# An own instruction order for the last of 32 periods in a windowed-attention block (one core, Trainium2)

## The reference, cut to what matters

```python
x = x + attention(_gn(x), ...)            # _gn: group norm, 32 groups, no affine part
# inside attention, 12 heads of 64:
qkv = x @ qkv_w.T + qkv_b                 # plus low-rank terms on q and v
attn = einsum('bqd,bkd->bqk', q * scale, k) + rel_h + rel_w     # 196 x 196 for each head
out = softmax(attn) @ v
return out @ proj_w.T + proj_b            # 768 -> 768, the output projection
```

## Time and profile before

| | |
|---|---|
| time, median of 3 runs | 3322.74 us (3322.59 to 3323.21) |
| the profiled execution | 3322.35 us |
| its span in the trace | 3320.5 us |
| PE busy | 3203.9 us, 96% of the span |
| DVE busy | 2750.2 us, 83% |
| ACT busy | 2124.7 us, 64% |
| mean granted TensorE clock | 0.981 |

### The profile page before, as it was taken

One profiled execution on the slowest core, in us unless ns is written; L12 is line 12 of the kernel. 1 busy time (PEld: TensorE's weight loads), 2 busy tenths in 40 slices (PEclk: granted clock), 3 DMA queues, 4 the chain that ended last, 5 costly groups with the idle time before them and its releaser, 6 DMA issues.

```text
span 3320.5 us, 78578 instructions
## 1 busy us (share of the span) xinstructions
PE 3203.9 (96%) x31280; PEld 1999.0 (60%) x31280; DVE 2750.2 (83%) x5490; ACT 2124.7 (64%) x5491; POOL 35.2 (1%) x65
## 2 busy tenths in 40 slices
PE   7489999999999999999999999999999999999997
PEld 4255666666666666666666666666666666666664
DVE  7688888888888888888888888888888888888874
ACT  3366666666666666666666666666666666666663
POOL 0100000000000000000000000000000000000000
PEclk6799999999999999999999999999999999999999
DMA  3157766567766666776666777666677666677654
GB/s 130 39 107 136 140 126 120 124 132 137 143 139 118 121 124 128 149 140 123 120 127 130 139 143 134 120 120 128 128 148 140 123 117 127 130 141 143 124 103 101
DMA packets 1267533, 420.09 MB, mean 127 GB/s; under 512 B 1092824, under 2 KB 1247448, under 8 KB 1267168
## 3 DMA queue, kind: packets, MB, share of 16 engines
q1 hardware_dynamic: 1251334, 377.69, 59.3%
q10 hardware_dynamic: 15834, 37.37, 3.8%
HBM read 86.60 MB, written 38.54 MB: 38 GB/s over the span
## 4 chain that ended last, share of the span: by engine, by line
PE 64%; DVE 22%; ACT 7%; issue 3%; DMA 1%; SPq 0%; POOL 0%; DVEq 0%; ACTq 0%; POOLq 0%
PE ring L554 34%; PE ring L621 14%; PE score L597 6%; DVE split L801 5%; ACT prob L686 5%; PE o_ps L611 5%; DVE sums L821 3%; DVE row_max L779 3%; PE ring L576 3%; PE ring L627 2%; DVE split L793 1%; DVE x_sb L845 1%; DVE k_lo L746 1%; DVE rel_sb L772 1%; DVE v_split L754 1%
## 5 line engine op out<-in xcount | busy, mean ns | idle before, releaser
L554 PE MATMUL ring<-xn,w_hi 128*128 128x392 f16 x6912 | 1713.0, 329 | 12.9 <-DMA xn<-xs 12.5
L554 PE MATMUL ring<-xn,w_lo 128*128 128x392 f16 x3456 | 1133.6, 328 | 0.0
L686 ACT ACTIVATE prob<-score,neg_max,exp_scale 98x196 f32<-98x196 f32 x1536 | 769.9, 510 | 306.4 <-DVE neg_max L783 303.2
L554 PEld LDWEIGHTS ring<-xn,w_hi 128*128 128x128 f16 x6912 | 643.1, 96 | 482.6 <-DMA xn<-xs 11.9
L801 DVE SCALAR_TENSOR_TENSOR split<-prob,row_inv,split 98x196 f16<-98x196 f32 x1536 | 545.6, 418 | 8.9
L779 DVE TENSOR_REDUCE row_max<-score 98x4 f32<-98x784 f32 x384 | 372.2, 969 | 165.4 <-PE score L597 165.3
L554 PEld LDWEIGHTS ring<-xn,w_lo 128*128 128x128 f16 x3456 | 331.8, 96 | 244.2 <-issue 2.9
L621 PE MATMUL ring<-o_hi,w_hi 128*128 128x392 f16 x1152 | 380.6, 330 | 1.4 <-DVE o_lo L810 1.4
L621 PE MATMUL ring<-o_hi,w_lo 128*128 128x392 f16 x1152 | 379.7, 330 | 0.0
L621 PE MATMUL ring<-o_lo,w_hi 128*128 128x392 f16 x1152 | 379.7, 330 | 0.0
L696 ACT ACTIVATE split<-prob,row_inv 98x196 f16<-98x196 f32 x768 | 310.2, 454 | 72.3 <-DVE row_inv L787 71.5
(11 more groups left out here) (114 smaller groups left out, 4494.8 us busy)
## 6 DMA issues: line engine op xcount, KB each, us to landing
y_sb<-in_x SPq DMA_DIRECT2D x192, 196.0 KB
out<-y_sb SPq DMA_DIRECT2D x192, 196.0 KB
x_sb<-in_x ACTq DMA_DIRECT2D x31, 1176.0 KB
rel_q<-rel_sb SPq DMA_DIRECT2D x128, 122.5 KB, 2.3
stage<-in_L_conv_qkv_w SPq DMA_DIRECT2D x3, 2304.0 KB, 15.0
turned<-split SPq DMA_TRANSPOSE x384, 4.2
rel_q<-rel_sb SPq DMA_DIRECT2D x128, 24.5 KB, 2.1
v_tok<-v_split SPq DMA_TRANSPOSE x192, 3.7
```

The lines of the kernel that those rows point to most:

```text
L554: last = T.matmul(ring[:, bank, 0:NT], w[:, c, 128 * j:128 * j + 128], xn[:, par, xx, :, c, 0:HALF], start=(c == 0 and part == 0), stop=(c ...
L686: last = A.activation(prob[:, head, half, :], score[0:HALF, head, TOK * half:TOK * half + TOK], ACT.Exp, bias=neg_max[:, k % 2, i:i + 1], ...
```

## The change

The last period with scores gets its own four tables (`PE_LAST`, `ACT_LAST`, `DVE_LAST`, `SP_LAST`), and periods 32 and 33 are gone.

1. `Y 3`, `Y 4`, `Y 5` of pair 30 move from slots 9, 10 and 11 to slots 4, 5 and 6, and `Z 3`, `Z 4`, `Z 5` to slots 5, 6 and 7. `V 5` moves from slot 10 and `K 5` from slot 9 to slot 8.
2. `Y` of pair 31 is cut in 36 pieces of three matmuls, `YC` with index 6 c + k: c is the head pair (the block that is summed over), k the output block. A piece waits for `o_lo` of its own head pair alone. Pieces of c = 0 to 4 and k = 0 to 4 (25 of them) stand in slots 9 to 11 and after `P 10`. Those of k = 5 follow, and those of c = 5 after `P 11`, with the transposes `Z` between them.
3. Blocks 0 to 4 use the five ring banks, block 5 and the first `Z` the two banks of `score`, the other `Z` the bank of the block before.
4. There are two buffers for the transposes' input: `yT`, and a part of `xs`, which is idle then.
5. For pair 31, x is loaded once as a whole to `x_sb` (step `LL`, 1176 KB, issued by ACT in slot 4); `Z` adds into it and the stores go out from there. Its six `LY` are gone.

```diff
+def chunks(c):
+    return [("YC", 0, 6 * c + k) for k in range(5)]
+PE_LAST = (
...
+    + each("S", 0, 4) + each("P", 0, 2) + each("Z", 1, 2) + each("K", 0, 3) + each("Y", 1, 3)
+    + each("S", 0, 5) + each("P", 0, 3) + each("V", 0, 3) + each("Y", 1, 4) + each("Z", 1, 3)
...
+    + each("S", 0, 11) + each("P", 0, 9) + chunks(3) + each("P", 0, 10) + chunks(4)
+    + each("YC", 0, 5, 11, 17, 23, 29)
+    + each("P", 0, 11) + each("YC", 0, 30, 31) + each("Z", 0, 0) + each("YC", 0, 32) + each("Z", 0, 1)
...
-    return [(kind, q - old, k) for q in range(-2, pairs + 2) for kind, old, k in order if 0 <= q - old < pairs]
+    return [(kind, q - old, k) for q in range(-2, pairs) for kind, old, k in (order if q < pairs - 1 else last)
+            if 0 <= q - old < pairs]
...
+    end = pairs - 1
+    bank["Y", end, CT - 1] = BANKS
+    bank["Z", end, 0] = BANKS + 1
+    for k in range(1, CT):
+        bank["Z", end, k] = bank["Y", end, k - 1]
...
+                elif kind == "YC":
+                    c, k = divmod(k, CT)
...
+                    if c == 0 and k == CT - 1:
+                        wait(pe, exps_done, 12 * pairs)
+                    wait(pe, o_lo_made, 6 * p + c + 1)
...
-                    wait(act, done["Z"], 6 * p + k)
-                    A.activation(yT[:, :], ring[:, bank, 0:NT], ACT.Identity,
+                    wait(act, done["Z"], 6 * p + (k - 1 if p == end and k > 0 else k))
+                    A.activation(yT_turns[k % 2 if p == end else 0], place(bank)[:, 0:NT], ACT.Identity,
...
+                if kind == "LL":
+                    wait(act, xs_lo_made, 2 * pairs)
+                    act.dma_start(x_sb[:, :, :], x_rows[p]).then_inc(x_in, 16)
...
+                elif kind == "Z" and p == end:
+                    wait(dve, done[kind], 6 * p + k + 1)
+                    wait(dve, x_in, 16 * (pairs + 1))
```

More of the change, by code:

```diff
@@ L128, with sequence @@
 PER_PAIR = {"Q": 6, "K": 6, "V": 6, "R": RCH, "Y": 6, "Z": 6, "G": 3}
-def sequence(order, pairs):
-    return [(kind, q - old, k) for q in range(-2, pairs + 2) for kind, old, k in order if 0 <= q - old < pairs]
+def sequence(order, pairs, last=()):
+    return [(kind, q - old, k) for q in range(-2, pairs) for kind, old, k in (order if q < pairs - 1 else last)
+            if 0 <= q - old < pairs]
 def ring_plan(pairs):
-    users = [step for step in sequence(PE_ORDER, pairs) if step[0] in PER_PAIR]
+    steps = [("Y", p, k) if kind == "YC" and k < CT - 1 else (kind, p, k)
+             for kind, p, k in sequence(PE_ORDER, pairs, PE_LAST)]
+    users = [step for step in steps if step[0] in PER_PAIR and step[:2] != ("Z", pairs - 1)]
     bank = {step: n % BANKS for n, step in enumerate(users)}
     user_before = {step: users[n - BANKS] for n, step in enumerate(users) if n >= BANKS}
+    end = pairs - 1
[3 more added lines that the diff above has]
+        bank["Z", end, k] = bank["Y", end, k - 1]
     return bank, user_before
@@ L485, in attend, with place @@
         normed, xs_hi_made, xs_lo_made, xn_in = sem("normed"), sem("xs_hi_made"), sem("xs_lo_made"), sem("xn_in")
+        last_out = sem("last_out")
+        yT_turns = [yT[:, :], xs[:, :, :, :].rearrange("p a b c -> p (a b c)").bitcast(F32)[:, 0:NT]]
         bank_of, user_before = ring_plan(pairs)
+        end = pairs - 1
+        def place(bank):
+            return ring[:, bank, :] if bank < BANKS else score[:, bank - BANKS, :]
         block = own.enter_context(nc.Block())
@@ L528, in _ @@
                                            ).then_inc(xn_in, 16)
+                elif kind == "ST" and p == end:
+                    wait(sp, read["Z"], 6 * p + k + 1)
+                    sp.dma_start(out_rows[p][:, :, 128 * k:128 * k + 128],
+                                 x_sb[:, :, 128 * k:128 * k + 128]).then_inc(last_out, 16)
                 elif kind == "ST":
@@ L535, in _ @@
             for slot in range(YS):
-                sp.wait_ge(y_out[slot], 16 * (CT // YS) * pairs)
+                sp.wait_ge(y_out[slot], 16 * (CT // YS) * end)
+            sp.wait_ge(last_out, 16 * CT)
         @block.tensor
         def _(pe):
-            for step in sequence(PE_ORDER, pairs):
+            for step in sequence(PE_ORDER, pairs, PE_LAST):
                 kind, p, k = step
@@ L623, in _ @@
                     last.then_inc(done[kind], 1)
+                elif kind == "YC":
+                    c, k = divmod(k, CT)
+                    y_step = ("Y", p, k)
+                    if c == 0 and k < CT - 1 and y_step in user_before:
+                        before, p_before, k_before = user_before[y_step]
+                        wait(pe, read[before], PER_PAIR[before] * p_before + k_before + 1)
+                    if c == 0 and k == CT - 1:
+                        wait(pe, exps_done, 12 * pairs)
+                    wait(pe, o_lo_made, 6 * p + c + 1)
+                    j = 3 * CT + k
+                    for part, (w, oo) in enumerate(((w_hi, o_hi), (w_hi, o_lo), (w_lo, o_hi))):
+                        last = T.matmul(place(bank_of[y_step])[:, 0:NT], w[:, c, 128 * j:128 * j + 128], oo[:, par, c, :],
+                                        start=(c == 0 and part == 0), stop=(c == HP - 1 and part == 2))
+                    if c == HP - 1:
+                        last.then_inc(done["Y"], 1)
                 elif kind == "Z":
                     wait(pe, read["Y"], 6 * p + k + 1)
+                    if p == end and k == 0:
+                        wait(pe, exps_done, 12 * pairs)
+                    from_yT = yT_turns[k % 2 if p == end else 0]
                     for i in range(4):
-                        last = T.transpose(ring[0:HALF, bank, 128 * i:128 * i + 128],
-                                           yT[:, HALF * i:HALF * i + HALF], ident[:, :])
+                        last = T.transpose(place(bank)[0:HALF, 128 * i:128 * i + 128],
+                                           from_yT[:, HALF * i:HALF * i + HALF], ident[:, :])
                     last.then_inc(done[kind], 1)
@@ L811, in _ @@
                                            o_hi[:, par, hp, :], ALU.add, ALU.subtract).then_inc(o_lo_made, 1)
+                elif kind == "Z" and p == end:
+                    wait(dve, done[kind], 6 * p + k + 1)
+                    wait(dve, x_in, 16 * (pairs + 1))
+                    y_cols = x_sb[:, :, 128 * k:128 * k + 128]
+                    V.tensor_tensor(y_cols, place(bank)[0:HALF, :].rearrange("p (a b) -> p a b", a=4),
+                                    y_cols, ALU.add).then_inc(read["Z"], 1)
                 elif kind == "Z":
```

53 lines of the change are left out of this document (49 added, 4 removed).

## The result

| | before | changed |
|---|---|---|
| median of 5 runs | 3323.10 us (3322.59 to 3324.18) | 3306.07 us (3304.87 to 3306.87) |
| ratio, with its 95% interval | 1 | 0.9947 (0.9935 to 0.9958) |
| span of the profiled execution | 3320.5 us | 3304.9 us |
| r4 in it (row maximum of slot 4) | 3232.43 | 3233.86 |
| from r4 to the end of the span | 88.1 us | 71.0 us |

The kernel is 17.0 us faster. Forecast was 3307.0, in the range 3304 to 3313. Everything the change touches lies behind r4; r4 itself came between 3231.1 and 3235.1 us in the traces of this study, by differences that lie ahead of it and so ahead of the change.

What follows compares the result with a forecast made beforehand. Bound: PE's matmuls or the softmax chain per slot, then a serial tail. Gain 19.3 less 2.2 gave span 3303.4; a likely clock fall made 3305.1, plus 1.85 and 0.39 makes 3307.3, stated as 3307.0, range 3304 to 3313.

Steps and rivals of the forecast that it cites:

- PE's groups (7.95, 7.51, 4.97): PE's matmul time in us: slots with S, P, V, Y, Z; slot 8; slot 7 without Y.
- the chain (5.54): Row maximum, exponentials, reciprocal and splits on DVE and ACT: 5.54 us per slot, 6.02 with a V split.
- The loss of 2.2 us up to r11: Slots 4 to 10: the row maximum of slot 11 comes 2.2 us later than before.
- The way from r11 to the end: From slot 11's row maximum to the span's end: 22.7 us instead of 42.0, a gain of 19.3.
- The wait before P 10: After slot 11's scores, P 9 and five pieces, PE waits 2.5 us for P 10's transpose.
- case-1: One clock fall in the wait before P 10, price 1.7 us: span 3305.1, time 3307.0; chance 0.45.
- case 2: The clock holds in the tail: span 3303.4, time 3305.6; chance 0.28.
- Case 3: Z 3 to Z 5 in slots 6 to 8 wait for x: 3320, or 3311 if one does; chance 0.15.
- Case 4: Clock goes down in slots 9 to 11 and stays down: 20 us more, 3325; chance 0.03.
- Terms at nothing: Counted as free: the x_sb load, semaphores, second buffer, SP's queue, moved Z sums; store queueing 0 to 1 us.
- that cover: A transpose slowed by the x_sb load hits P 4, which stands two slots of 7.95 us later.
- Case 5: A piece waits for a bank or `o_lo` in PE's queue: 3 to 8 us less gain, 3310 to 3315; chance 0.09.

Runs made afterwards that it cites:

- filled kernel: Changed kernel with four of the five pieces of block 5 moved from behind P 10 to ahead of it; 3305.34 us.
- pieces-only kernel: Kernel before with its old order of slots 0 to 11, and behind it all that is new for pair 31; 3324.29 us, ratio 1.0003.
- without x_sb: Changed kernel with pair 31's x in six loads through the two y_sb buffers instead of one load; 3317.92 us, ratio 0.9986.
- pair 30 early only: Kernel before with item 1 of the change alone, pair 31 in whole blocks; 3322.95 us, ratio 0.9999.
- the one built on it: Filled kernel with the pieces of c = 1 in slot 10 and three pieces instead of two ahead of the first Z; 3305.88 us.
- the pieces alone, with their waits mended: Pieces-only kernel with x_sb loaded in slot 2 and pair 30's last load ahead of the last transpose on SP; 3313.52 us, ratio 0.9974.
- spread: The one built on it, with the last two pieces of block 5 behind P 11; 3303.72 us, ratio to before 0.9942.

## Why the prediction was right, point by point

**Slots.** r7, r8, r9, r10 and r11 were worked out at 23.9, 29.9, 36.7, 42.8 and 48.3 us from r4; they came at 23.9, 29.9, 36.5, 42.8 and 48.4, and to 0.02 us the same in each kernel with these slots. That PE's groups (7.95, 7.51, 4.97) and the chain (5.54) add up like this is shown. The loss of 2.2 us up to r11, counted against the gain, is there (48.4 against 46.1). One count in it was wrong and changed no term: ahead of r11 stand 45 matmuls of pair 31, the pieces of c = 0 to 2, and not 75.

**The way from r11 to the end.** 22.7 worked out, 22.65 measured. The wait before P 10 was 2.1 us and not 2.5: P 10 came 9.7 after r10 instead of 9.9, and PE was free 7.6 after it instead of 7.4. P 11 started 9.9 after r11 (3292.12 - 3282.25), as taken, but with no wait before it, so by PE's own list and not by its transpose; the sum had the two 0.1 us apart. In the filled kernel, where P 11 does wait for its transpose, it starts 9.8 after r11. The steps behind it: 2.0 to the first projection, 7.6 from there to the end of the last sum, and 3.15 from there to the end instead of 2.8. The forecast's total of 10.6 holds 7.8 for the first stretch, but its terms (5.5, 0.68, 0.14, 0.61 and 0.69) add up to 7.6, so this slip of 0.2 hid most of the 0.3 that the stores took more. In the other traces with these six stores this last stretch took 2.85 to 3.24 us; how much of it is stores behind each other is not shown.

**The clock, cases 1 and 2.** I forecast the fall as likelier (0.45 against 0.28) and priced it at 1.7 us. It fell in three of five traces and cost 1.6 to 1.7; the first profiled execution was one of the others. The span of the second, 3304.8, is the case-1 number (3305.1), that of the first is case 2's 3303.4 plus the 1.4 by which its r4 came late: that it agrees with case 1 is luck. The median of 3306.07 lies between 3305.6 and 3307.3 and can't say more, as r4 of the two traces of this kernel lies 1.5 us apart. Whether the clock falls in an execution was not foreseen, only what it costs.

**Case 3, loads of x as the wait.** No sum for pair 30 waited for a load in the changed kernel. The wait is real, though: 5.62 us of DVE in the pieces-only kernel, which held PE for 4.86, and 2.7 to 4.7 four times without x_sb. The new order escapes it by issuing each load a slot ahead and by not needing six of them.

**Case 4, the clock in the thin tail.** Its full form (20 us) did not come in the changed kernel. In part it exists: with pair 30 early only the clock was low for 23.9 us on end, from the end of slot 9 through slots 10 and 11, which then hold no pieces, and on past P 11, and behind P 11 it fell in the filled kernel and the one built on it. My argument against it, that a low stretch of 3.4 us ended in full work, holds only while there is such work. What the Trainium skill warns of ("TensorE: Matmul & The Clock Gate", section "A second HAM failure mode: psum-queue depth-cycling") is small idles between groups of matmuls that make the clock go down and up again and again, where case 4 has it stay down. It has rows here on both sides: 1.00 and then 0.50 in the filled kernel's tail, one fall and not many, and 1.00 throughout in the tail of the changed kernel, with idles of 0.27 to 1.35 us.

**Terms at nothing.** The load of x_sb cost nothing because P 4 started 10.1 us after its transpose was issued (3249.66 against 3239.58), and this took 8.2 us to land. The pieces-only kernel is the cover taken away: slots of 6 us, a wait of 2.42, r7 2.8 late and r11 2.2. I named that cover and then left it out of my expectation for that kernel. Case 5 (a piece held by a bank) did not come in the changed kernel and did in that one.

## What to carry to other kernels

A tail that runs serially is shortened by splitting its products along the summed dimension, so that all but the last part runs before the last input is there; but it needs free accumulators, and so the older work out of the way first: the pieces alone, with their waits mended, gave 9 of the 17 us, the early move alone nothing. Before moving work to the end of a list, look at what each of its first waits stands for on the other lists: a load queued behind a transpose, together with a transfer that had lost its cover, undid all 9. Count from the last event that the change leaves alone; differences of a few tenths show there that run times with a spread of 2 us hide.

## What the runs showed of the hardware

A wait of PE of 2.1 us between stretches of full work brought the granted clock from 1.00 to 0.50 in three of five traces and not in two, though the wait lay at the same place in all. The fall came at the end of the wait or up to 0.9 us behind it, when PE was at work again. Waits of 1.35 to 1.5 us alone did not bring it down. It fell 0.5 us behind the wait of 2.42 (pieces only), and 0.6 us behind a wait of 0.48 and one of 1.35 with only P 11 between them (filled kernel), and 0.4 us behind the same pair (0.47 and 1.35) in the kernel built on it; spread, with 1.47 and 0.24 around P 11, kept it. No experiment varied these waits alone, so what brings it down there is open. With full work behind it the low stretch lasted 3.4 us; with more waits in it 6.8 and 23.9 us. A low stretch of 3.4 us costs 1.6 to 1.7 us of a PE-bound path. I had not expected that filling one wait would only move the fall to the next place where PE does little.
